# A GRU and its expert layer on one core: one transposition of the gates' sums, and gate activations first in ScalarE's steps

## What is computed

```python
def cell(h, x):
    gi = x @ W_ih + b_ih
    gh = h @ W_hh + b_hh
    i_r, i_z, i_n = jnp.split(gi, 3, axis=-1)
    h_r, h_z, h_n = jnp.split(gh, 3, axis=-1)
    r = jax.nn.sigmoid(i_r + h_r)
    z = jax.nn.sigmoid(i_z + h_z)
    n = jnp.tanh(i_n + r * h_n)
    h_new = (1.0 - z) * n + z * h
    return (h_new, h_new)
...
probs = jax.nn.softmax(x @ w_gate, axis=-1)
topk_w, topk_ids = jax.lax.top_k(probs, 2)
...
routed = jnp.einsum('te,eth->th', combine, eo)          # 8 experts, inner width 256
shared = _silu_and_mul(x @ w_sh_gate_up) @ w_sh_down    # inner width 1024
return x + routed + shared
```

## Time and profile before

| what | us |
|---|---|
| median of 3 runs | 1204.74 |
| lowest and highest | 1201.41, 1206.31 |
| the profiled execution | 1195.19 |
| its span, from the first to the last instruction | 1193.4 |

### The profile page before, as it was taken

The page is one execution under the profiler, slowest core; times in us unless marked ns, Lnnn a source line. Parts: engine busy times, 40 slices in busy tenths (PEclk is TensorE's granted clock), DMA queues, the critical chain, the costliest instruction groups (busy, mean ns, idle before and its releaser), DMA issues.

```text
span 1193.4 us, 35909 instructions
## 1 busy us (share of the span) xinstructions
PE 1036.9 (87%) x13452; PEld 623.1 (52%) x13452; DVE 850.0 (71%) x4089; ACT 573.3 (48%) x1877; POOL 206.2 (17%) x213
## 2 busy tenths in 40 slices
PE   2789888889999898999899989998998898889894
PEld 2556555556665454555455545554555454555452
DVE  5898999868889888677867787678787778721111
ACT  4755555655555543445344434443444444435442
POOL 0200011020110212111211121112120112233332
PEclk9999999999999999999999999999999999999897
DMA  8943455381864753623451234234342144488694
GB/s 307 402 147 97 144 180 186 107 205 56 294 237 173 197 193 73 230 75 61 125 178 29 55 101 166 56 55 174 129 126 55 28 143 134 121 296 278 181 288 56
DMA packets 68829, 183.13 MB, mean 153 GB/s; under 512 B 7737, under 2 KB 40288, under 8 KB 61344
## 3 DMA queue, kind: packets, MB, share of 16 engines
q1 hardware_dynamic: 45632, 107.74, 25.5%
q0 software_dynamic: 23024, 73.11, 23.1%
HBM read 137.01 MB, written 52.87 MB: 159 GB/s over the span
## 4 chain that ended last, share of the span: by engine, by line
PE 51%; DVE 27%; ACT 10%; issue 7%; DMA 3%; POOL 0%; POOLq 0%; SPq 0%; ACTq 0%; DVEq 0%
PE psG L715 17%; PE psG L721 14%; PE psU L778 6%; DVE arena L1046 5%; DVE arena L1044 5%; ACT arena L1429 4%; ACT arena L1425 4%; PE psS L824 3%; DVE arena L1054 3%; DVE arena L1069 3%; DVE arena L1065 3%; DVE arena L1056 3%; PE psD L790 3%; DVE arena L1048 2%; PE psO L845 2%
## 5 line engine op out<-in xcount | busy, mean ns | idle before, releaser
L715 PE MATMUL psG<-arena 128*32 128x384 f16 x4096 | 213.8, 329 | 76.1 <-DVE arena L1069 68.2
L1425 ACT ACTIVATE arena<-arena 128x32 f32<-128x32 f32 x256 | 58.6, 229 | 336.7 <-DVE arena L1048 335.3
L721 PE MATMUL psG<-arena 128*32 128x384 f16 x4096 | 211.9, 327 | 3.7 <-issue 3.7
L778 PE MATMUL psU<-arena 128*128 128x256 f16 (+1 forms) x1920 | 203.7, 253 | 0.2 <-DVE arena L940 0.2
L1044 DVE STREAM_TRANSPOSE arena<-psG 128x128 f32<-128x128 f32 x256 | 81.1, 317 | 144.8 <-PE psG L721 138.2
L778 PEld LDWEIGHTS psU<-arena 128*128 128x128 f16 x1920 | 157.7, 99 | 49.1 <-issue 13.6
L715 PEld LDWEIGHTS psG<-arena 128*32 128x32 f16 x4096 | 86.2, 96 | 175.0 <-DVE arena L1069 141.9
L1625 POOL DMA_INDIRECT y<-arena x55 | 87.6, 1593 | 393.4 <-DVE arena L1046 312.2
L721 PEld LDWEIGHTS psG<-arena 128*32 128x32 f16 x4096 | 109.9, 97 | 60.9 <-issue 4.4
L1046 DVE STREAM_TRANSPOSE arena<-psG 128x256 f32<-128x256 f32 x256 | 104.1, 407 | 0.0
L790 PE MATMUL psD<-arena 128*128 128x512 f16 x384 | 97.6, 382 | 4.9 <-DVE arena L1264 4.9
(11 more groups left out here) (166 smaller groups left out, 1557.7 us busy)
## 6 DMA issues: line engine op xcount, KB each, us to landing
arena<-expert_weights SPq DMA_DIRECT2D x39, 1536.0 KB, 8.6
arena<-wgu POOLq DMA_DIRECT2D x32, 512.0 KB, 5.5
...
```

What stands on the lines that cost most here:

```text
L715: e.matmul(psG[32 * j:32 * j + 32, 0:384], prev[:, c, 2:6].rearrange("p q n -> p (q n)"), whv[c][1][:, :, :, 32 * j:32 * j + 32], start=(c ...
L721: r = e.matmul(psG[32 * j:32 * j + 32, 0:384], prev[:, c, 0:4].rearrange("p q n -> p (q n)"), whv[c][0][:, :, :, 32 * j:32 * j + 32], star ...
L778: r = e.matmul(psU[u % 2][:, 256 * gu:256 * gu + width], half(W_GS + ex * 4 + c, pw)[:, o:o + 128], hh[:, 1 - ph, c, first:first + width], ...
L1425: e.activation(Ur, Ur, ACT.Tanh, scale=reg_tr).then_inc(th_r, 1)
```

## The change

Four things are edited. All three gates' sums (384 columns) are turned by one transposition, L1053 in the new file, which waits for step_mm and placed and raises turned_g; the sum of r behind it waits for turned_g, as do warm, GpSimd's waits and one wait of the expert blocks. In the plan, s_gate and e_gate come ahead of ScalarE's other pieces of their step. What needs a gate's result may stand in the same step; a gate that needs a result of VectorE stands a step later. And route of a group waits in the plan for record of the group before.

```diff
--- before.py
+++ after.py
@@ -89,6 +89,8 @@
     TAIL = {"PE": 1.4, "DVE": 1.4, "ACT": 1.5, "SP": 99.0, "POOL": 2.0}
     KEPT = {"PE": 0.35, "DVE": 0.3, "ACT": 0.3, "SP": 0.0, "POOL": 2.0}
 
+    EARLY = ("s_gate", "e_gate")
+
     INDEXED, ISSUE = ("file", "rows", "hidden", "add", "s_add"), 2.7
     RANK = {"PE": 0, "DVE": 1, "ACT": 2, "SP": 3, "POOL": 3}
 
@@ -114,6 +116,10 @@
             return 1 + int(self.LANDS[a[0]] / (3.9 if t < T else 1.25))
         if here == there:
             return 0
+        if a[0] in self.EARLY:
+            return 0
+        if name[0] in self.EARLY and here == "DVE":
+            return 1
         if a[0] in ("sw_low", "ew_low") and there == "ACT":
             return 1
         if there in ("SP", "POOL"):
@@ -158,6 +164,8 @@
             saved = room
             t += 1
             assert t < 900, left[:20]
+        for names in self.at["ACT"].values():
+            names.sort(key=lambda n: n[0] not in self.EARLY)
         self.step_of, self.steps = done, t
 
     def of(self, engine, t):
@@ -237,7 +245,7 @@
         due = s - 3 if n == 2 else s - 40
         last = [("rank", g - 1)] if g else []
         p.add("PE", ("logits", g), 0.5 * n, last + [("scales", 0)], step=s, due=due, takes=True)
-        p.add("DVE", ("route", g), 0.25 + 0.45 * n, [("logits", g)], due=due, frees=True)
+        p.add("DVE", ("route", g), 0.25 + 0.45 * n, [("logits", g)] + ([("record", g - 1)] if g else []), due=due, frees=True)
         p.add("ACT", ("route_w", g), 0.3, [("route", g)], due=due)
         p.add("DVE", ("choose", g), 0.75, [("route", g)], due=due)
         listed = [("list", i, 0) for i in range(STATIC) if group_of(i) == g - 1]
@@ -542,8 +550,8 @@
         gi_mm, gi_ev_a, gi_ev_v, bias_ready, h_start, router_w = (
             sem(s) for s in ("gi_mm", "gi_ev_a", "gi_ev_v", "bias_ready", "h_start", "router_w"))
 
-        step_mm, tr_r, tr_zn, red_r, red_n, red_z, g_q, g_w, g_zc, g_zh, g_m, g_H, g_hi, g_lo = (
-            sem(s) for s in ("step_mm", "tr_r", "tr_zn", "red_r", "red_n", "red_z", "g_q", "g_w", "g_zc", "g_zh", "g_m",
+        step_mm, turned_g, red_r, red_n, red_z, g_q, g_w, g_zc, g_zh, g_m, g_H, g_hi, g_lo = (
+            sem(s) for s in ("step_mm", "turned_g", "red_r", "red_n", "red_z", "g_q", "g_w", "g_zc", "g_zh", "g_m",
                              "g_H", "g_hi", "g_lo"))
         th_r, th_z, th_n, placed, kept = (sem(s) for s in ("th_r", "th_z", "th_n", "placed", "kept"))
 
@@ -819,7 +827,7 @@
                     if k == 0:
                         e.wait_ge(gi_ev_a, 12 * NBLK - 6)
                     if k == KS + 1:
-                        e.wait_ge(tr_zn, T)
+                        e.wait_ge(turned_g, T)
                 for j, (ph, pw) in enumerate(PROD):
                     r = e.matmul(up_bank(k)[:, 0:512], hT[k % 2][:, ph, c], ew_half(k, c, pw),
                                  start=(c == 0 and j == 0), stop=(c == KC - 1 and j == 2))
@@ -848,7 +856,7 @@
                     r.then_inc(e_dn, 1)
 
             def warm(t, n):
-                e.wait_ge(tr_zn, t + 1)
+                e.wait_ge(turned_g, t + 1)
                 for _ in range(n):
                     e.matmul(psG[:, 0:384], trih, whv[0][0][:, :, :, 0:32], start=True, stop=True)
 
@@ -1041,12 +1049,10 @@
                 e.wait_ge(step_mm, t + 1)
                 if t == 0:
                     e.wait_ge(h_start, 2)
-                e.transpose(Tt[:, 0:4, 0:32], psG[:, 0:128].rearrange("p (f m) -> p f m", m=32)).then_inc(tr_r, 1)
                 e.wait_ge(placed, t + 1)
-                e.transpose(Tt[:, 4:12, 0:32], psG[:, 128:384].rearrange("p (f m) -> p f m", m=32)).then_inc(tr_zn, 1)
-                e.wait_ge(tr_r, t + 1)
+                e.transpose(Tt[:, :, 0:32], psG[:, 0:384].rearrange("p (f m) -> p f m", m=32)).then_inc(turned_g, 1)
+                e.wait_ge(turned_g, t + 1)
                 e.tensor_reduce(U3[:, 0:4], Tin[:, 0:4, 0:B], AX.X, ALU.add).then_inc(red_r, 1)
-                e.wait_ge(tr_zn, t + 1)
                 e.tensor_reduce(U3[:, 8:12], Tin[:, 8:12, 0:B], AX.X, ALU.add).then_inc(red_n, 1)
                 e.tensor_reduce(U3[:, 4:8], Tin[:, 4:8, 0:B], AX.X, ALU.add).then_inc(red_z, 1)
                 e.wait_ge(th_r, t + 1)
```

## The result

The changed kernel takes 1249.25 us (median of 4 runs, 1248.99 to 1251.04) beside 1205.53 us for the kernel before (4 runs): a ratio of 1.037, 95% interval 1.034 to 1.040, 44 us more. I had predicted 1231, in a range up to 1239. The direction was right, the size was not.

A forecast was written before the change was run, and what follows sets the result against it. The bound was taken as each recurrent step's chain, with TensorE waiting for h, not TensorE's work. Loop +18 and tail +9 make +27 on the 1204.7 us median, rounded to 1231 us; range 1203 to 1239.

The forecast's parts named there:

- The transposition: VectorE's merged transposition of 384 columns in each step: 579 ns taken, bounds 497 and 579.
- Rivals 1 and 3: Merged transposition's price. 1: grows by 90 ns, chance 0.17; 3: middle price 538 ns, 1214 to 1222 us, chance 0.13.
- The wait: r's sum, waiting for the merged transposition, starts 0.03 us behind its end, at 0.61 us instead of 0.57.
- Rival 2: Waiting on the operation just ahead costs nothing; 0.07 us saved in a step, 18 over the loop, 1187 us; chance 0.03.
- The sum behind it: r's sum on VectorE behind the transposition: 246 ns, bounds 218 and 246; with the later start, +0.07 us a step.
- nothing hides it: Loop step: the next step's matmuls wait for h nearly always, so the +0.07 us only lengthens that wait.
- Gates first inside the loop: Gates ahead of ScalarE's other pieces in the loop's steps: priced at 0, bounds -1 and +2 us.
- The tail: Gates first behind the loop: net +9 us, bounds -7 and +14.
- The prediction's own pattern: Blocks 32 to 34 behind the loop: TensorE idle 4.8 us per three blocks instead of 1.6; five patterns, +16 us.
- A slower pace hides part of it, I say 5: Blocks 26 to 29 already wait for accumulating DMAs; a slower pace hides 5 us of the tail's loss.
- Less the 2 us moved into the loop: Three pieces of 0.6 us leave the tail, some 2 us of TensorE's work, deducted from the +16.
- Rival 4: Loop as forecast, but the tail gains, no gate standing behind a turn_out: -7 + 18, 1216 us; chance 0.12.

The follow-up runs named there:

- swap: Kernel before, with z's and n's 256 columns transposed first, r's 128 second, and r's sum waiting for the second; ratio 1.026.
- wait_alone: Kernel before, with one wait changed: r's sum waits for the second transposition instead of the first; 1239.61 us, ratio 1.028.
- filled: Merged transposition with the plan of before, plus an operation without a use between transposition and r's sum; 1222.59 us, ratio 1.012.
- turn_alone: Changed kernel with the plan of before, so the merged transposition and its wait alone; 1221.59 us, ratio 1.014.
- plan_alone: Changed kernel with the two transpositions of before, so the new plan of work alone; 1228.70 us, ratio 1.021.
- loop_only: Kernel before's two transpositions, with the new plan rules and gates-first sort only in the loop's steps; 1210.61 us, ratio 1.002.
- flip_back: Changed kernel with one thing undone: s_add 13 stands behind both file 9 again in GpSimd's list; 1238.78 us, ratio 1.036.

## Why the prediction was right, and where it was wrong

**The transposition: right.** 582 ns beside 579, and by the reason given: swap shows the 133 ns for each 128 columns. The Trainium skill, "Vector Engine (DVE) Microarchitecture Reference", section 3.8, with its one element per cycle and lane, and VectorE's 0.96 GHz, which the Trainium skill gives in "VectorE: DVE Perf Modes", section "The TRN2 errata", make an estimate of 133 ns for 128 columns; the rows agree (132 to 134 ns), once they are compared at one place in the queue. Rivals 1 and 3 fall with it.

**The wait: right in kind.** The sum starts 0.617 - 0.582 = 0.035 us behind the end (0.03 predicted). Rival 2 falls: wait_alone pays 0.154 us a step for a wait on the operation just ahead. The Trainium skill, "VectorE: DVE Perf Modes", section "The DRAIN you can't avoid", found no extra cost of a semaphore after each of eight copies; that doesn't carry over to this step. filled shows what is free here: the slot in the wait, for something that needs nothing.

**The sum behind it: mis-sized, by little.** The prediction gave it 246 ns, with 218 and 246 as bounds; it lasts 260, outside them. 0.046 us of later start and 0.042 of a longer row give a step that is 0.087 us longer, where +0.07 stood. The bound came from L1050, which doesn't stand behind a wait; no row of before did in this form. 255 such steps make +22 us. In the whole time turn_alone shows 17 us of it (15 to 20), and the +18 of the prediction lies inside; that it does is in part luck, since a step that was too short met stalls that shrank, and the prediction had said that nothing hides it.

**Gates first inside the loop: right.** 0 predicted, plan_alone's step is 3.810 beside 3.809 us, and loop_only's whole time is 1.002.

**The tail: this is the step that failed.** It was given +9 us; plan_alone costs 24 us in the whole time (1228.70 beside 1204.47), and the two profiles differ by 25.7. By the starts of the turns, relative to the loop's end, before and after:

| term | before | after | difference | predicted |
|---|---|---|---|---|
| loop's end to turn 23 | 31.3 | 37.2 | +5.9 | not seen |
| fifteen blocks without the hole | 94.9 | 111.2 | +16.3 | +16 - 2 |
| the hole at blocks 29 to 31 | 6.6 | 11.3 | +4.7 | -5 |
| turn 38 to the end | 24.9 | 23.6 | -1.3 | 0 |
| sum | 157.6 | 183.3 | +25.7 | +9 |

The holes stand where the sum had them, but for the one ahead of up 33: 22.14 us for a pattern instead of 21.39; the 0.75 are act_t 32 behind turn_out 33 (0.3) and down 34, whose act_out stands behind out 33 on ScalarE (0.4).

That +16 was met to 0.3 us is in part luck. The prediction's own pattern lasts 21.39 us against 3 x 6.47 = 19.41, which makes +2.0 for each and +10 for five; it counted the idle time instead, +3.2 for each, as if a pattern held the work of three blocks. It holds less: 3 matmuls of s_down and 39 of units in the pattern above, where blocks 32 to 34 of before have 6 and 48. Measured, the last four patterns are 2.6 us longer each, 10.4 in all, and the first, turns 23 to 25, is 5.8 longer (22.76 beside 16.91 us, a stretch that was short before and was taken at 19.4).

Three steps failed. "A slower pace hides part of it, I say 5" was only a guess with a sign: the hole didn't shrink in any kernel with the new order behind the loop (7.8 us in plan_alone, 11.3 in after, 6.6 in before). In after the accumulation in it took 11.89 us instead of 7.72, and out (L1528) on ScalarE stood for the landing, while the weights' loads now came in pairs; how much of the 4.7 us in the table is that and how much the scatter between executions stays open. "Less the 2 us moved into the loop" counted TensorE's work, which isn't what bounds the tail, as I had said of the table one line earlier. And the stretch to turn 23 was priced at nothing without being looked at, though two lists had changed there: file 9 behind s_add 13 on GpSimd, s_up 64 ahead of record on VectorE. Against before's profile it is 5.9 us longer, against the other traces with the plan of before 3.5 to 4.9. Rival 4 (the tail gains) falls.

The sum with the terms of the two profiles is 22 + 26 = 48 us; medians give 44, of which turn_alone has 17 and plan_alone 24. flip_back, from an occasion on which the kernel before took what its profile shows (1195.1 and 1195.2), has 22.8 us in the loop and 22.3 in the tail, 45 in all, and its medians differ by 43.7.
